# One step for the V products of a head group, inverse deviations on ScalarE, four more C products on GpSimd, and new orders

## What is computed

```python
xn = ln(h)                                       # (B, L, 256), L = 512
scores = einsum('bqhd,bkhd->bhqk', q, k) * 16**-0.5      # 16 heads of 16, causal
attn_out = softmax(scores) @ v @ o_w + o_b
x_c = silu(conv4(xn @ in_proj_w[:, :512]) + conv_b)
dt = softplus(x_dbc[..., :16] @ dt_w + dt_b)
h = exp(dt * A) * h + (x_c * dt) * B_t           # per step; 512 channels x 16 states
y = sum over states of C_t * h
ssm = ((y + x_c * D) * silu(z)) @ ssm_out_w
x1 = x + alpha * attn_out + (1 - alpha) * ssm;  x1 + gelu(ln(x1) @ w1) @ w2
```

## Time and profile before

| | us |
|---|---|
| median of 3 runs (5196.34 to 5197.73) | 5196.59 |
| the profiled execution | 5201.05 |
| its span, first to last instruction | 5199.2 |
| PE busy, 96% | 4974.5 |
| DVE busy, 91% | 4751.3 |
| POOL busy, 89% | 4629.3 |
| ACT busy, 77% | 4016.0 |
| mean granted TensorE clock, share of 2.4 GHz | 0.989 |

### The profile page before, as it was taken

The page is one execution under the profiler, slowest core; times in us unless marked ns, Lnnn a source line. Parts: engine busy times, 40 slices in busy tenths (PEclk is TensorE's granted clock), DMA queues, the critical chain, the costliest instruction groups (busy, mean ns, idle before and its releaser), DMA issues.

```text
span 5199.2 us, 94534 instructions
## 1 busy us (share of the span) xinstructions
PE 4974.5 (96%) x32280; PEld 3447.1 (66%) x32280; DVE 4751.3 (91%) x7332; ACT 4016.0 (77%) x6403; POOL 4629.3 (89%) x2925
## 2 busy tenths in 40 slices
PE   5899999999999999999999999999999999999997
PEld 2567666667666667666677667677666676666665
DVE  4999999999999999999999999999999999999984
...
GB/s 150 159 152 154 158 166 160 163 156 154 163 161 164 159 163 148 164 167 158 160 153 159 167 167 160 156 152 159 170 161 158 155 155 162 160 164 159 161 141 55
DMA packets 522016, 812.29 MB, mean 156 GB/s; under 512 B 80976, under 2 KB 227832, under 8 KB 521536
## 3 DMA queue, kind: packets, MB, share of 16 engines
...
q10 hardware_dynamic: 4768, 0.28, 0.1%
...
## 4 chain that ended last, share of the span: by engine, by line
PE 71%; DVE 10%; issue 8%; POOL 6%; DMA 2%; ACT 1%; SPq 1%; DVEq 0%; POOLq 0%; ACTq 0%
PE pY L984 12%; PE pM L1133 9%; PE pM L1145 8%; PE pM L1026 4%; PE pM L1120 4%; PE pM L1060 4%; DVE pD L1262 4%; PE pM L1073 4%; PE pM L993 4%; PE pM L1006 3%; POOL state L600 3%; PE pM L1093 3%; PE pM L1034 2%; PE pM L1117 2%; PE pM L1041 2%
## 5 line engine op out<-in xcount | busy, mean ns | idle before, releaser
L600 POOL TENSOR_TENSOR state<-scan_in,bc 128x1024 f32<-128x1024 f32 x1024 | 2406.7, 2363 | 145.4 <-PE pY L984 136.5
L745 ACT ACTIVATE pD<-scan_in,A 128x512 f32<-128x512 f32 x2048 | 1404.4, 690 | 401.5 <-DVE state L1270 315.9
L1262 DVE TENSOR_TENSOR_SCAN pD<-pD,state 128x512 f32<-128x512 f32 x1280 | 1545.2, 1219 | 69.0 <-ACT pD L745 67.7
L984 PE MATMUL pY<-ident,state 128*128 128x128 f32 x8192 | 1153.2, 275 | 32.4 <-POOL state L588 25.0
L588 POOL TENSOR_TENSOR state<-state,bc 128x512 f32<-128x512 f32 x768 | 969.6, 1274 | 155.8 <-DVE state L1262 155.8
L984 PEld LDWEIGHTS pY<-ident,state 128*128 128x128 f32 x8192 | 907.9, 142 | 267.8 <-issue 108.7
L1301 DVE TENSOR_REDUCE mx<-pM 128x1 f32<-128x512 f32 (+3 forms) x1408 | 860.1, 630 | 154.7 <-PE pM L1075 146.7
L1262 DVE TENSOR_TENSOR_SCAN state<-pD,state 128x512 f32<-128x512 f32 x768 | 916.4, 1210 | 57.7 <-ACT pD L745 57.6
L846 ACT ACTIVATE region<-pM 128x512 f32<-128x512 f32 (+1 forms) x1408 | 741.7, 559 | 177.8 <-PE pM L1095 153.9
L1270 DVE TENSOR_TENSOR state<-pD,bc 128x512 f32<-128x512 f32 x1280 | 862.1, 680 | 11.0
L1073 PE MATMUL pM<-region 96*128 96x512 bf16 (+3 forms) x2048 | 521.4, 301 | 24.8 <-DVE region L1318 12.1
...
## 6 DMA issues: line engine op xcount, KB each, us to landing
bc<-bc_d SPq DMA_DIRECT2D x2048, 256.0 KB, 3.9
...
qk_d<-qkp SPq DMA_DIRECT2D x64, 384.0 KB, 3.4
qk_d<-ht SPq DMA_DIRECT2D x64, 384.0 KB, 5.1
...
region<-qk_d SPq DMA_DIRECT2D x256, 64.0 KB, 3.1
...
```

The costliest lines, as they stand in the source:

```text
L600: nc.gpsimd.tensor_tensor(state[:, at_:at_ + JP], us[:, parity(b), k // N * JP:(k // N + 1) * JP, :], bc[:, k % BC_SLOTS, 0, :].unsqueeze( ...
L745: act.activation(pD[DECAY_BANK[e]][:], dts[:, parity(b), j], ACT.Exp, scale=A[:, j, n:n + 1]).then_inc(a_ok.sem, 1)
L984: ins = pe.matmul(y_part(t, e % JP), state[:, e % RING, t * P:(t + 1) * P], ident[:], is_transpose=True, start=False, stop=(e % PASS >= PA ...
L1262: v.tensor_tensor_scan(h if e in POOL_C else decay, decay, h, 0.0, ALU.mult, ALU.add)\
```

## The change

- V products: `probs_v` makes all four key blocks of a group in one step `pv{g}`, 16 products behind one wait for all the group's exponentials. `probs` has four buffers: two as before, a new tile `probs2` for block 2, and `oT` for block 3, whose exponential thereby waits for the transposes of the group before (for group 0: the last output product).
- Inverse deviations: new steps `l0r` to `l3r` on ScalarE, a logarithm, an exponential and a copy with scale -1. GpSimd keeps one product (`l0s` to `l3s`). The set that holds both functions is loaded right behind each large activation.
- `POOL_C` has 28 members, so VectorE has 36 C products.
- The opening: batch 0's first steps follow lists of their own (`EARLY`), then the rest of the table. Its four q/k splits have a tile each (`qk_first`), and its `xp` no longer waits for them.
- `w_xp` has 80 columns instead of 128, `w_dt` half as many.
- The tables `ORDER` and `PLACE` are new throughout.

```diff
-POOL_C = [e for e in range(SCANS) if e // JP % 4 == 3 or e % (4 * JP) == 2 * JP - 1]
+POOL_C = [e for e in range(SCANS) if e // JP % 4 == 3 or e % (4 * JP) == 2 * JP - 1 or e % (8 * JP) == 4 * JP + 1]
...
+        probs.append(sb("probs2", [P, G, L - 2 * P]))
         shared = at[0]
+        qk_first = region[:, shared:shared + 4 * L].rearrange("p (n t) -> p n t", n=4)
         oT = view(L)
+        probs.append(oT.rearrange("p (h t) -> p h t", h=G))
...
+            opening = [(name, 0) for name, shift in order if shift > 0]
+            opening += [(name, shift) for name, shift in order if shift >= 0]
+            for name in early:
+                opening.remove((name, 0))
+            for name, n in [(name, 0) for name in early] + opening:
+                step(name, Batch(None, n))
+            for n in range(1, B):
+                turn(Batch(None, n), False, n == B - 1)
...
-                b.wait(pool, mv[n])
-                nc.gpsimd.tensor_tensor(rst[:], mvt[:, :, 1], eps4[:], ALU.add).then_inc(ve[n].sem, 1)
-                nc.gpsimd.tensor_tensor(nmt[:], mvt[:, :, 0], mone4[:], ALU.mult).then_inc(nm[n].sem, 1)
-                b.wait(pool, ve[n])
-                nc.gpsimd.tensor_tensor(rst[:], rst[:], mhalf4[:], ALU.pow).then_inc(rs[n].sem, 1)
+                _, mvt, _, nmt = lns[n]
                 b.wait(pool, rs[n])
-                b.wait(pool, nm[n], 1)
-                nc.gpsimd.tensor_tensor(nmt[:], nmt[:], rst[:], ALU.mult).then_inc(nm[n].sem, 1)
+                nc.gpsimd.tensor_tensor(nmt[:], mvt[:, :, 0], nmt[:], ALU.mult).then_inc(nm[n].sem, 1)
...
+            def rstd(b, n):
+
+                _, mvt, rst, nmt = lns[n]
+                b.wait(act, mv[n])
+                act.activation(rst[:], mvt[:, :, 1], ACT.Ln, bias=eps4[:, 0:1]).then_inc(ve[n].sem, 1)
+                b.wait(act, ve[n])
+                act.activation(rst[:], rst[:], ACT.Exp, scale=-0.5).then_inc(rs[n].sem, 1)
+                b.wait(act, rs[n], 1)
+                act.activation(nmt[:], rst[:], ACT.Copy, scale=-1.0).then_inc(rs[n].sem, 1)
...
+                    if b.off:
+                        b.wait(act, qk_lo)
...
                     act.activation(gT(b), gT(b), ACT.Gelu).then_inc(g_ok.sem, 1)
+                    act.preload_act_table_set(EXP_LN)
...
-                    if h == 0:
-                        if g * TB + kb >= 2:
-                            b.wait(act, pv_ok, g * TB + kb - 1)
+                    if kb == 0 and h == 0:
+                        if g:
+                            b.wait(act, pv_ok, g)
                         else:
-                            b.wait_last(act, pv_ok, NG * TB + kb - 1)
-                    act.activation(probs[kb % 2][:, h:h + heads, 0:n],
+                            b.wait_last(act, pv_ok)
+                    elif kb == TB - 1:
+                        if g:
+                            b.wait(act, ot_ps, g)
+                        else:
+                            b.wait_last(act, out_ps)
+                    act.activation(probs[kb][:, h:h + heads, 0:n],
...
-            def probs_v(b, g, kb):
-
-                made = p_exp, scores_after(g, kb, G - HEADS[kb])
-                if kb == 0:
+            def probs_v(b, g):
+
+                if g == 0:
                     b.wait(pe, v_ok)
-                    next_bank(f"pv{g}_0", b, o_ev, g + 1, made)
-                else:
-                    b.wait(pe, *made)
-                pO = pM[bank_of(f"pv{g}_0")]
-                for h in range(G):
-                    ins = pe.matmul(pO[32 * h:32 * h + HD + 1, kb * P:L], vt[:, kb, g * G + h, :],
-                                    probs[kb % 2][:, h, 0:L - kb * P], start=(kb == 0), stop=(kb == TB - 1),
-                                    skip_group_check=True)
+                pO = next_bank(f"pv{g}", b, o_ev, g + 1, (p_exp, (g + 1) * STS))
+                for kb in range(TB):
+                    for h in range(G):
+                        ins = pe.matmul(pO[32 * h:32 * h + HD + 1, kb * P:L], vt[:, kb, g * G + h, :], probs[kb][:, h],
+                                        start=(kb == 0), stop=(kb == TB - 1), skip_group_check=True)
                 ins.then_inc(pv_ok.sem, 1)
...
-        st3_2_0 pv3_1 st3_2_2 st3_3_0 add59 pv3_2 pv3_3 +v1 on3 add60 add61 add62 ot0 ot1 add63 +z0 +skip0 yt0 yt1
...
+        st3_1_3 +mx0_2 add56 +v0 st3_2_0 +mx0_3 add57 add58 st3_2_2 st3_3_0 add59 pv3 add60 add61 on3 +z0 add62 ot0
...
+EARLY = {engine: text.split() for engine, text in {
+    "SP": "load qk0 qk1 xp qk2 rb0 rc0 rb1 rc1 qk3 ld0 l1a",
+    "POOL": "l0s l0a l0b l0c l1s qr0 ql0 qr1 ql1 qr2 ql2 u0 fill0 qr3 ql3 fill1 u1",
+    "ACT": "l0r l0a l1r l1a xt0 xt1 xs0 xs1 xs2 xs3 qk0 xsilu qm0 qk1 qm1 qk2 xp dt0 dt1 qm2 dt2 dt3 sp2 qk3 qm3",
+    "PE": "xt0 xt1 xs0 xs1 xs2 xs3 qk0 qk1 qk2 xp dt0 dt1 dt2 dt3 qk3",
+    "DVE": "l0s l1s xs0 xs1 xs2 xs3",
 }.items()}
```

189 lines of the change are left out of this document (100 added, 89 removed).

## The result

The changed kernel takes 5223.68 us (median of 5 runs, 5216.52 to 5227.47) where the kernel before took 5196.59. The ratio is 1.0047, with a 95% interval of 1.0036 to 1.0058: 0.5% slower, where 1.8% faster was forecast. Its profiled execution took 5227.05, of which the span is 5225.2.

What follows compares the result with a forecast made beforehand. TensorE was taken to bound the kernel. Savings of 3.1 us a turn over 31 turns (96), +3 for the opening and -1 for inverse deviations took 5201.05 to 5107; less 4.5 to the median, 5103, range 5065 to 5150.

Steps and rivals of the forecast that it cites:

- So TensorE sets the pace: Steady turn: TensorE, busy 153.89 of 156.80 us, bounds it, with VectorE 6 and GpSimd 9 us behind.
- the saving of 2.0: V products on TensorE: 4 separate runs a turn instead of 13 save 9 x 0.22 = 2.0 us a turn.
- the 0.8 of waits: TensorE's waits for exponentials ahead of V products: 1.3 us a turn, of which 0.8 is saved.
- The sum's line of 96 us: Steady turns: savings of 2.0, 0.8 and 0.3 make 3.1 us a turn, times 31 turns.
- weight loads show: Rival: weight loads at 12 block boundaries inside V runs cost 1.1 us a turn, giving 5138; chance 0.05.
- row of maxima: TensorE's wait for the DMA of that row: 0.3 us a turn saved, bounds 0 and 0.46.
- the 0.5 that was left for `pv3`: Wait ahead of group 3's V step, with only four transposes before it: 0.5 us a turn remains.
- C products and inverse deviations: Engine loads a turn: VectorE 145.0, GpSimd 144.3, ScalarE 128.6 us; nothing on the path from ScalarE's added work.
- the slower rival: Inverse deviations block ScalarE, delaying decays at four places; a turn 1.9 us longer, 5259; chance 0.12.
- GpSimd or VectorE takes the bound: Rival: at GpSimd's present share a turn takes 156.3 us, 1.0 less than now, giving 5168; chance 0.15.
- The opening: Start of the kernel: first scan near 102, 6 us later; the following turn 2.9 us shorter, VectorE 94.9% busy.
- The net of +3: Later first scan and shorter following turn together: 3 us added, bounds -12 and +10.

Runs made afterwards that it cites:

- `b_less`: Kernel before with the V products of key blocks 1 to 3 computed on only a quarter of their columns; 5210.39 us, ratio 1.0026.

## Why the prediction was wrong, point by point

**"So TensorE sets the pace": this step failed.** It was read from the windows of a whole turn and from the chain's 71%. Both are right as averages. But TensorE is without a gap, and has the chain, only in 77 of 157 us, and even there 6.9 us less for it gave 0.15 a turn, since ScalarE's evictions, GpSimd's 19.9 us of work in 20.6 and a falling clock stood close behind. In the other 80 VectorE is busier and TensorE has gaps. Since all V products stand in the 80, the saving of 2.0, and the 0.8 of waits with it, could not pass into the turn. The run `b_less` shows it in the kernel before: 3.5 us less for TensorE, nothing gained, and 0.2 a turn where the clock stayed full. The sum's line of 96 us was 0 for its main term.

**A term that the sum lacked.** The prediction took the new order to leave TensorE's other products alone; of `xp` and `dt` it looked only at the width. `dt2` and `dt3`, no longer side by side, are the larger part of 1.4 us a turn that the `dt` products cost TensorE more, and its work fell by 0.1 in all, not by the 2.0 of the V products. So even where TensorE does set the pace there was almost nothing to pass on. What this alone costs in time wasn't measured.

**V products: the term's size was right.** Four runs a turn, each 2.37 us by the prediction's count where some 2.4 were expected, 0.2 lost in each, and no cost at the boundaries. The rival "weight loads show" did not happen.

**Waits inside attention, row of maxima.** The wait ahead of group 3's step fell from about 0.95 a turn to 0.4 (13.4 us, 31 times in TensorE's waits of the kernel after):

```profile
PE pM L1038 <- ACT region L878: 13.4, 31, 0.5
```

which is the 0.5 that was left for `pv3`. But the sum had no term for waits that the new order makes: the banks of `mx3_0` and `st3_1_3`, the load of group 3's Q and K and the late C row were there to be read in the order. They turned out to cost next to nothing (banks) and 12 us (row); the load wasn't tried. That they were not looked for was an error, though not the one that decided.

**C products and inverse deviations.** Loads right within 1.4 us on VectorE, GpSimd and ScalarE. An inverse deviation on ScalarE takes 0.78 us, from 1061.42 to the end at 1062.20 in ScalarE's timeline of the kernel after, and 0.8 was expected:

```profile
1061.42 0.30 ACT L704 ACTIVATE ln_rs<-ln_mv,eps 128x4 f32<-128x4 f32 x1 [1.82 <-DVE ln_mv L1237]
1061.75 0.20 ACT L706 ACTIVATE ln_rs<-ln_rs 128x4 f32<-128x4 f32 x1
1061.99 0.21 ACT L708 ACTIVATE ln_nm<-ln_rs 128x4 f32<-128x4 f32 x1
```

ScalarE does wait for the statistics (116.3 us over the span), as the slower rival said. But VectorE's waits for decays did not grow: 95.2 + 21.1 us after, 57.6 + 67.7 before. The time came out on the slower side without that rival's mechanism, which had put it at 5259.

**The rival "GpSimd or VectorE takes the bound"** was nearest in kind: VectorE is the busiest in the middle. But it too treated the turn as one stretch with one bound, and so expected the turn to be 1.0 us shorter.

**The opening.** Silu was expected at 59 and starts at 60.41, the end of softplus at 77 (79.52), the first scan at 102 (101.66). The step that failed is what should follow: batch 0's turn was to be 2.9 us shorter, since the first scans would find all ready, and is 1.7 longer, with VectorE busy for 135.78 of 148.20, 91.6% instead of the assumed 94.9%. The net of +3 was +7.2, inside its bounds. Why that turn is longer stays open.
